# Router logits taken from widened products with the search moved forward, and the experts' inner layer produced transposed from copied weights

## The chip, the cores and the metric

The kernel runs on one core of one Trainium2 chip. The metric is device time in microseconds of one execution, the median of three runs. All arithmetic of interest is fp32. In the rows PE is TensorE (its weight loads are a row of their own, PEld), DVE is VectorE, ACT is ScalarE, POOL is GpSimd, and SP is the engine that issues most transfers.

## The reference, cut to what matters

The input is 8 sequences of 1024 tokens with 128 channels. An attention layer over each sequence is followed by a state-space layer, and then by a mixture of 8 experts of which each token takes the best 2. What the change touches is the end of the second layer and the third:

```python
t = t + _L1_attn_ref(_ln_t(t), ...)      # ends in: x + einsum('ble,de->bld', y, W_out), y 256 wide
t = t + _L1_ffn_ref(_ln_t(t), ...)
# _L1_ffn_ref, on n = 8192 tokens of 128 channels, 8 experts, inner width 341
logits = flat @ router_w.T
probs = softmax(logits); topk_probs, topk_idx = top_k(probs, 2)
topk_probs = topk_probs / (sum(topk_probs) + 1e-09)
h1 = einsum('nc,ehc->neh', flat, w1); h3 = einsum('nc,ehc->neh', flat, w3)
h = silu(h1) * h3
y = einsum('neh,ech->nec', h, w2); out = einsum('ne,nec->nc', gates, y)
```

`_ln_t` is a normalisation over channels, (v - mean) / sqrt(var + 1e-5).

## The kernel before, in words

Every engine runs its own instruction list, written out by hand; semaphores order them, and nothing but the order in the code and the waits decides who runs when.

**The batch stage.** The 8192 tokens are 64 tiles of 128 rows, in 8 batches (sequences) of 8 tiles. `batches` calls `step(base, i)` for 79 steps, `i` from 0 to 7 and `base` the first tile of the batch. A step is a software pipeline: it does the scores of tile i (L346 to L348), the softmax on ACT (L613), the attention output of tile i-1 (L427), the input products of the second layer for tiles i-3 and i-4 (L354, L357, L467, L469), the state-space work of tile i-6 and the end of that layer for tile i-7 (L371 to L375, the output product L432, the residual sum `T2`, L1155). Its mean and variance (L1162, L1183) give `rs2` in `norm_for_experts` on POOL, once a batch at the end of step 6.

**The router.** The finished batch is searched two batches after its first tile. In step 7 and in step 0 ACT normalises its 8 tiles into `XA` (`normed`, L691). In step 0 PE transposes them (`rows_of_x`, L310, two times four into the bank `pc`), ACT copies each half to `VT` (L696), and PE multiplies each tile by the router's weights (`logits`, L316, eight products of 8 columns, each of two instructions). DVE copies the result (L1196) at the end of step 0. In step 1 come the maximum and the softmax (`below_max`, `shares`), the best values (`best`, L948) and their indices (`best_index`, L955); in step 2 the one-hots and gates and, on PE, the counts (L444, L447); in step 3 the rows' places (`places`, `rows`). Then POOL scatters the 16 tiles by `scatter_rows` (L896) to `rows_by_expert` in DRAM, spread over steps 3 to 1 of the next batch by the table `SPREAD`, whose key is (step, place in the step).

**The tables.** After the last step DVE works out which expert each of 136 slots of 128 rows belongs to (L1228 to L1252); the experts of six slots are packed into one number in `TBI`.

**The expert stage.** A loop over 136 slots, four to a loop turn (`group`). SP fetches the slot's rows (`GX`, L273). For slot n PE does, in this order: h1 (L520, the transposed rows stationary, the expert's 341 columns of `W1` moving, into `pX`), the transpose of slot n+1's rows (L509), the three transposes of the gated h of slot n-1 (L529), h3 (L522, likewise with `W3`, into `pY`), and the result of slot n-2 (L537, three chunks of the inner width, `HT` times `W2`). Every fp32 product is two instructions with two weight loads, a transpose is one. ACT copies the transposed rows (L706), takes silu(h1) (L710) and scales the result by the gate (L719). DVE multiplies silu(h1) by h3 (`gated`, L1257), copies the transposed h from `pc` to `HT` (`turned`, L1261), and takes the row numbers and gates (L1268, L1269). POOL scatters each result (L908). At the start of a loop turn PE reads the packed number (`experts_of`) to address `W1`, `W3` and `W2`. At the end SP loads the results back and DVE adds them (L1285, L1287).

## Time and profile before

| | us |
|---|---|
| median of 3 runs (lowest, highest) | 1275.35 (1275.05, 1277.6) |
| the profiled execution's own time | 1275.21 |
| its span, first to last instruction | 1273.4 |
| batch stage and the router's tail, about | 0 to 885 |
| tables and fetch of the first rows, about | 885 to 912 |
| expert stage, about | 912 to 1229 |
| results back, sums, stores, about | 1229 to 1273 |
| mean granted TensorE clock | 0.942 of full |

The profile shows one execution. Busy shares of PE are not a measure of its limit, since its instructions overlap in the records: what counts is the distance from one start to the next. The waits name who released an engine, the chain of waits follows back from the last instruction what each step waited for.

### The profile page before, as it was taken

How to read it: one execution, taken by the hardware profiler on the slowest of the kernel's cores; microseconds unless marked ns; L12 is line 12 of the kernel's file. 1: busy time of each engine (PE TensorE's matmuls, PEld its weight loads, DVE VectorE, ACT ScalarE, POOL GpSimd, SP SyncE). 2: the span in 40 equal slices, each digit the busy share in tenths (PEclk: the TensorE clock that was granted, in tenths of full speed). 3: DMA queues.
4: the chain of work that ended last, by engine and by line, in shares of the span. 5: the costliest groups of instructions: out<-in, count | busy, mean ns of one | idle time of the engine just before them, and what ended most of it. 6: DMA issues, size and time to landing. Idle time of an engine off the chain costs nothing.

```text
span 1273.4 us, 28242 instructions
## 1 busy us (share of the span) xinstructions
PE 1108.5 (87%) x7784; PEld 963.3 (76%) x7785; DVE 866.5 (68%) x2843; ACT 702.8 (55%) x1748; POOL 601.8 (47%) x860
## 2 busy tenths in 40 slices
PE   3899999999999999999999998872399999999950
PEld 2689889888888888888888888762288888888740
DVE  2578887888877887887888777754255555555534
ACT  1576776667767677676666666622144444444420
POOL 7123342564565466556457465555444444444320
PEclk8999999999999999999999999875699999999975
DMA  7100000001001001001000000001222222222249
GB/s 216 28 1 26 10 2 26 18 16 37 17 13 39 8 23 39 10 23 39 5 22 15 18 12 14 12 11 34 55 59 58 58 58 58 58 58 58 57 119 305
DMA packets 73174, 55.21 MB, mean 43 GB/s; under 512 B 9797, under 2 KB 67693, under 8 KB 73069
## 3 DMA queue, kind: packets, MB, share of 16 engines
q1 hardware_dynamic: 55437, 32.15, 9.6%
q0 software_dynamic: 8448, 17.45, 4.3%
q10 hardware_dynamic: 9184, 4.33, 1.2%
q8 instruction: 51, 0.84, 0.3%
q14 instruction: 54, 0.44, 0.1%
HBM read 31.21 MB, written 23.22 MB: 43 GB/s over the span
## 4 chain that ended last, share of the span: by engine, by line
PE 53%; DVE 14%; POOL 12%; issue 12%; ACT 5%; DMA 2%; SPq 1%; POOLq 0%; DVEq 0%; ACTq 0%
PE pX L520 6%; PE pY L522 6%; PE pc L371 5%; PE pa L427 4%; PE pb L537 4%; PE pd L537 4%; PE pc L529 4%; POOL rows_by_expert L896 3%; DVE CV L1020 2%; PE pY L333 2%; ACT PR L613 2%; POOL st L878 2%; DVE NM L1041 2%; PE pc L375 1%; PE pa L382 1%
## 5 line engine op out<-in xcount | busy, mean ns | idle before, releaser
L908 POOL DMA_INDIRECT results_by_choice<-YE,DIX x136 | 130.5, 960 | 190.7 <-ACT YE L719 178.4
L1261 DVE COPY V<-pc 128x384 f32<-128x384 f32 x136 | 75.8, 558 | 133.4 <-PE pc L529 132.1
L896 POOL DMA_INDIRECT rows_by_expert<-XA,SL x128 | 142.3, 1112 | 38.0 <-issue 28.1
L371 PEld LDWEIGHTS pc<-XDT,M 128*128 128x128 f32 x1024 | 130.1, 200 | 17.9 <-issue 13.4
L1020 DVE SCALAR_TENSOR_TENSOR CV<-XBC,cw,CV 128x256 f32<-128x256 f32 x288 | 140.5, 540 | 0.2 <-issue 0.2
L371 PE MATMUL pc<-XDT,M 128*128 128x64 f32 x1024 | 127.7, 280 | 10.7 <-DVE OFF L998 10.0
L427 PE MATMUL pa<-V,PT 128*128 128x128 f32 x1024 | 128.1, 278 | 3.6 <-DVE XDT L1077 3.5
L839 POOL TENSOR_TENSOR YG<-Y,SZ 128x256 f32<-128x256 f32 x64 | 46.5, 726 | 172.2 <-DVE Y L1062 170.0
L427 PEld LDWEIGHTS pa<-V,PT 128*128 128x128 f32 x1024 | 120.0, 192 | 9.6 <-issue 5.7
L520 PE MATMUL pX<-W,TA 128*128 x272 | 104.4, 465 | 0.9 <-ACT TA L706 0.7
L522 PE MATMUL pY<-W,TA 128*128 x272 | 101.1, 454 | 0.0
L1041 DVE TENSOR_REDUCE NM<-pX 128x1 f32<-128x1024 f32 x64 | 77.9, 1218 | 33.2 <-PE pX L348 31.5
L585 ACT ACTIVATE PT<-pY 128x1024 f32<-128x1024 f32 x64 | 65.6, 1025 | 52.3 <-PE pY L333 52.3
L1257 DVE TENSOR_TENSOR X<-XT,pY 128x341 f32<-128x341 f32 x136 | 69.4, 510 | 31.4 <-PE pY L522 19.6
L613 ACT ACTIVATE PR<-pX,NM 128x1024 f32<-128x1024 f32 x64 | 70.8, 1107 | 19.8 <-DVE NM L1041 19.7
L1138 DVE TENSOR_TENSOR M<-ED,GT 128x1024 f32<-128x1024 f32 x64 | 78.3, 1224 | 3.0 <-ACT ED L634 2.7
L706 ACT ACTIVATE TA<-pa 128x128 f32<-128x128 f32 x136 | 37.8, 278 | 74.5 <-PE pa L509 74.5
L333 PE MATMUL pY<-ident,PR 128*128 128x128 f32 x512 | 68.3, 277 | 1.5 <-ACT PR L613 1.5
L529 PE MATMUL pc<-ident,X 128*128 128x128 f32 (+1 forms) x408 | 66.9, 273 | 0.0
L537 PEld LDWEIGHTS pb<-W,V 128*128 128x128 f32 (+1 forms) x408 | 56.1, 191 | 14.0 <-issue 1.1
L537 PEld LDWEIGHTS pd<-W,V 128*128 128x128 f32 (+1 forms) x408 | 56.1, 191 | 12.9
L529 PEld LDWEIGHTS pc<-ident,X 128*128 128x128 f32 (+1 forms) x408 | 50.5, 145 | 20.4 <-DVE X L1257 0.6
(250 smaller groups left out, 2902.9 us busy)
## 6 DMA issues: line engine op xcount, KB each, us to landing
GX<-rows_by_expert SPq DMA_DIRECT2D x136, 65.0 KB
XT<-in_xT_dram SPq DMA_DIRECT2D x8, 512.0 KB, 3.9
X<-in_x_dram SPq DMA_DIRECT2D x16, 256.0 KB, 3.0
W<-results_by_choice SPq DMA_DIRECT2D x8, 512.0 KB, 8.7
out_dram<-T ACTq DMA_DIRECT2D x8, 512.0 KB, 7.3
results_by_choice<-YE,DIX POOLq DMA_INDIRECT x136, 2.2
rows_by_expert<-XA,SL POOLq DMA_INDIRECT x128
W<-in_w1T_dram SPq DMA_DIRECT2D x1, 1364.0 KB
```

Of the source, the lines that this page charges most:

```text
L333: last = nc.tensor.transpose(pY[:, P * j:P * j + P], PR[:, P * j:P * j + P], ident[:])
L371: mm(pc[:, 64 * h:64 * h + 64], M[:, h, :], XDT[:, e % 2, HD * h:HD * h + 64], start=h == 0, stop=False, skip_group_check=True)
L427: last = mm(pa[:, 0:C], PT[:, P * j:P * j + P], V[:, j, :], start=j == 0, stop=j == NT - 1)
L520: mm(pX[:, 512 * par:512 * par + HID], GXT[:, par, :], W1[:, cols], start=True, stop=True).then_inc(s("h1_ps"), 1)
L522: mm(pY[:, 512 * par:512 * par + HID], GXT[:, par, :], W3[:, cols], start=True, stop=True).then_inc(s("h3_ps"), 1)
L529: last = nc.tensor.transpose(pc[0:hn, P * k:P * k + P], HH[:, par, h0:h0 + hn], ident[:])
L537: last = mm((pd, pb)[par][:, 0:C], HT[0:hn, par, k, :], W2[0:hn, bass.ds(expert, 1), k, :], start=k == 0, stop=k == len(HC) - 1)
L613: A(PR[:], pX[:], ACT.Exp, bias=NM[:, i:i + 1], accum_out=RS[:, i:i + 1]).then_inc(s("exp_ready"), 1)
L896: g.indirect_dma_start(xg, bass.IndirectOffsetOnAxis(ap=SL[:, j // NT, j % NT:j % NT + 1], axis=0), XA[:, j // NT, j % NT, :], None).then_ ...
L908: g.indirect_dma_start(yg, bass.IndirectOffsetOnAxis(ap=DIX[:, j, :], axis=0), YE[:, j, :], None).then_inc(s(f"ye{j}_scattered"), 16)
L1020: return stt(CV[:, m, :], XBC[:, m, fo + tap:fo + tap + 256], cw[:, m, tap:tap + 1], CV[:, m, :], ALU.mult, ALU.add)
L1041: v.tensor_reduce(NM[:, i:i + 1], pX[:], AX.X, ALU.max, negate=True).then_inc(s("nm_ready"), 1)
```

## The change

It has three parts.

1. *The logits.* The router's weights become 8 more columns of two products that are done anyway: of `wz` (z of the normalised input, 264 to 272 columns) and of `wo` (the layer's output product, 128 to 136 columns; the 8 are W_out times the router's weights, worked out once in step 3 of the first batch, with two transposes, five small products and three DVE copies, for the first of which PE waits). DVE scales the 8 columns per tile (`XR`, and `LR` beside the residual sum), and in step 7 turns them into logits with the mean and the variance of the normalisation (`logits`, `centred`, `logits_max`, `below`). `rows_of_x`, the old `logits`, `VT`, both ACT copies and the DVE copy of `LG` go.
2. *The search moved forward.* Logits, maximum and exponential run in step 7, the sums, shares and best values in step 0, the indices stay in step 1, the rest in steps 2 and 3. `norm_for_experts` is split, seven tiles ahead of POOL's own `norm` of step 6 and one behind it; the scatters of `SPREAD` lie at fewer places, all behind the small POOL operations of `RY`; `normed` of step 0, `TR`, `take_q` and `take_ql` change their place in the order. `st` gets two buffers.
3. *The experts.* h1 and h3 come out transposed: the weights are stationary (three chunks of 128, 128 and 85 columns) and the 128 transposed rows move. The weights are first copied to a static place `WS`, `W1`'s 341 columns by ACT and `W3`'s by DVE, for each slot; both read the packed number for it. `hidden_T` and `turned` go, the gated product is written straight to `HT` (384 columns), and the result of slot n-1 follows h3 of slot n.

```diff
-            def rows_of_x(base, grp):
-            def logits(base):
...
-                    mm(pb[:, 0:DI + H], XNT[:, 0:P], wz[:], start=True, stop=True).then_inc(s("z_ps"), 1)
+                    mm(pb[:, 0:DI + H + E], XNT[:, 0:P], wz[:], start=True, stop=True).then_inc(s("z_ps"), 1)
...
-                        last = mm(pb[:, 0:C], YT[:, m, :], wo[:, m, :], start=m == 0, stop=m == 1)
+                        last = mm(pb[:, 0:C + E], YT[:, m, :], wo[:, m, :], start=m == 0, stop=m == 1)
...
+                if base == 0 and i == 3:
+
+                    for m in range(2):
+                        last = nc.tensor.transpose(pd[:, P * m:P * m + P], wo[:, m, 0:C], ident[:])
+                    last.then_inc(s("woT_ps"), 1)
+                    pe.wait_ge(s("woT_ready"), 1)
+                    for m in range(2):
+                        mm(pd[:, 256 + E * m:256 + E * m + E], SQ[:, P * m:P * m + P], rT[:], start=True, stop=True, skip_group_check=True)
+                    mm(pd[:, 256 + 2 * E:256 + 3 * E], ones[:], rT[:], start=True, stop=True, skip_group_check=True).then_inc(s("woR_ps"), 1)
...
-                if routes:
-                    upto(pe, "vT_ready", base, -12)
-                    rows_of_x(base, 1)
...
-                if routes:
-                    logits(base)
...
-            def hidden(n, par, expert, between):
+            def hidden(n, par, between):
 
                 pe.wait_ge(s("gxt_ready"), n)
-                cols = bass.ds(expert * HID, HID)
-                mm(pX[:, 512 * par:512 * par + HID], GXT[:, par, :], W1[:, cols], start=True, stop=True).then_inc(s("h1_ps"), 1)
+                pe.wait_ge(s("w1_ready"), n)
+                for k, (h0, hn) in enumerate(HC):
+                    last = mm(pX[0:hn, 512 * par + P * k:512 * par + P * k + P], WS[:, par, 0, h0:h0 + hn], GXT[:, par, :], start=True, stop=True, skip_group_check=True)
+                last.then_inc(s("h1_ps"), 1)
                 between()
-                mm(pY[:, 512 * par:512 * par + HID], GXT[:, par, :], W3[:, cols], start=True, stop=True).then_inc(s("h3_ps"), 1)
-
-            def hidden_T(n, par):
+                pe.wait_ge(s("w3_ready"), n)
+                for k, (h0, hn) in enumerate(HC):
+                    last = mm(pY[0:hn, 512 * par + P * k:512 * par + P * k + P], WS[:, par, 1, h0:h0 + hn], GXT[:, par, :], start=True, stop=True, skip_group_check=True)
+                last.then_inc(s("h3_ps"), 1)
...
+            def weights(par, expert):
+
+                A(WS[:, par, 0, :], W1[:, bass.ds(expert * HID, HID)], ACT.Copy).then_inc(s("w1_ready"), 1)
...
-            SPREAD = {(3, 3): (0, 1), (4, 1): (2,), (4, 2): (3,), (5, 1): (4,), (5, 2): (5,), (6, 1): (6,), (6, 2): (7,),
-                      (7, 1): (8,), (7, 2): (9,), (7, 3): (10,), (0, 1): (11,), (0, 2): (12,), (0, 3): (13,), (1, 1): (14,), (1, 2): (15,)}
+            SPREAD = {(3, 3): (0, 1), (4, 2): (2, 3), (5, 2): (4, 5, 6, 7), (7, 2): (8, 9, 10), (0, 2): (11, 12), (1, 2): (13, 14, 15)}
...
+                        ts(XR[:, (fb + j) % NT, :], bank[:, DI + H:DI + H + E], st[:, fpar, 6, j:j + 1], st[:, fpar, 6, 2 + j:3 + j], ALU.mult, ALU.mult)
...
+                    stt(LR[:, e % NT, :], pb[:, C:C + E], RY[:, 1, 0:1], XR[:, e % NT, :], ALU.mult, ALU.add)
...
-                tt(HH[:, par, :], SH[:, par, :], pY[:, 512 * par:512 * par + HID], ALU.mult).then_inc(s("hh_ready"), 1)
-
-            def turned(n, par):
-                dve.wait_ge(s("hT_ps"), n)
-                v.tensor_copy(HT[:, par].rearrange("p k t -> p (k t)"), pc[:, 0:P * len(HC)]).then_inc(s("hT_ready"), 1)
+                tt(HT[:, par].rearrange("p k t -> p (k t)"), SH[:, par, :], pY[:, 512 * par:512 * par + HP3], ALU.mult).then_inc(s("hh_ready"), 1)
+
+            def weights(par, expert):
+
+                v.tensor_copy(WS[:, par, 1, :], W3[:, bass.ds(expert * HID, HID)]).then_inc(s("w3_ready"), 1)
```

## Rows read from the trace of the kernel before

**Rows 1.** The page: busy time by engine, and the chain that ended last by engine.

```profile
PE 1108.5 (87%) x7784; PEld 963.3 (76%) x7785; DVE 866.5 (68%) x2843; ACT 702.8 (55%) x1748; POOL 601.8 (47%) x860
PE 53%; DVE 14%; POOL 12%; issue 12%; ACT 5%; DMA 2%; SPq 1%; POOLq 0%; DVEq 0%; ACTq 0%
```

**Rows 2.** Busy time in windows: window, length, each engine, PE clock, DMA share, GB/s.

```profile
199.90:203.40 3.50, 3.50 (x13) 2.92 (x12) 1.90 (x5) 2.26 (x6) 2.01 (x5) 0.52 0.00 0
202.64:690.78 488.14, 468.29 (x3552) 421.39 (x3551) 407.07 (x1364) 340.03 (x808) 272.01 (x408) 0.99 0.06 21
...
920.00:1240.00 320.00, 305.57 (x1882) 246.18 (x1880) 162.52 (x539) 132.89 (x401) 130.50 (x136) 0.98 0.24 63
```

**Rows 3.** Timeline of DVE: start and length of L1041, which runs once a step.

```profile
90.66 1.23 DVE L1041 TENSOR_REDUCE NM<-pX 128x1 f32<-128x1024 f32 x1
103.25 1.23 DVE L1041 TENSOR_REDUCE NM<-pX 128x1 f32<-128x1024 f32 x1 [0.57 <-PE pX L348]
185.71 1.22 DVE L1041 TENSOR_REDUCE NM<-pX 128x1 f32<-128x1024 f32 x1
202.62 1.23 DVE L1041 TENSOR_REDUCE NM<-pX 128x1 f32<-128x1024 f32 x1 [1.49 <-PE pX L348]
690.76 1.21 DVE L1041 TENSOR_REDUCE NM<-pX 128x1 f32<-128x1024 f32 x1
```

**Rows 4.** Chain of waits, two stretches: start, length, engine, tile, line, instructions.

```profile
195.43 0.44 PE pc L310 x4
196.73 1.83 PE pc L316 x16
...
938.12 0.67 PE pd L537 x6
```

**Rows 5.** Timeline of PE in the expert stage, one slot, the first of a loop turn.

```profile
1050.21 0.83 PE L520 MATMUL pX<-W,TA 128*128 x2
1050.88 0.27 PE L509 MATMUL pa<-ident,GX 128*128 128x128 f32 x1
1050.99 0.49 PE L529 MATMUL pc<-ident,X 128*128 128x128 f32 x3
1051.32 0.74 PE L522 MATMUL pY<-W,TA 128*128 x2
1051.89 0.83 PE L537 MATMUL pd<-W,V 128*128 x6
1052.56 0.74 PE L520 MATMUL pX<-W,TA 128*128 x2
```

**Rows 6.** Single lines: count, shortest/median/longest ns, first and last start.

```profile
L520 PEld LDWEIGHTS pX<-W,TA x272: 186/190/333, 913.4 to 1221.6; 128*128 128x128 f32 x136
L686 ACT ACTIVATE XA<-XA x8: 1043/1050/1057, 223.0 to 880.1; 128x1024 f32<-128x1024 f32 x8
L1209 DVE TENSOR_SCALAR wx<-wx,pcol x1: 407/407/407, 19.5 to 19.5; 128x384 f32<-128x384 f32 x1
L1054 DVE TENSOR_TENSOR dts<-pb,hrow x32: 147/156/160, 51.9 to 819.9; 128x8 f32<-128x8 f32 x32
```

**Rows 7.** Expert stage by line: busy us, mean ns, then idle before and its releasers.

```profile
L908 POOL DMA_INDIRECT results_by_choice<-YE,DIX x136 | 130.5, 960 | 190.7 <-ACT YE L719 178.4 <-issue 12.2
...
L1261 DVE COPY V<-pc 128x384 f32<-128x384 f32 x134 | 74.7, 558 | 132.2 <-PE pc L529 130.9 <-issue 1.3
L1257 DVE TENSOR_TENSOR X<-XT,pY 128x341 f32<-128x341 f32 x134 | 68.4, 510 | 11.7
L710 ACT ACTIVATE XT<-pX 128x341 f32<-128x341 f32 x133 | 59.9, 450 | 0.2 <-PE pX L520 0.2
```

**Rows 8.** Waits of the batch stage, 90 to 800 us: total us, times, longest.

```profile
PE pb L405 <- POOL YG L839: 12.7, 8, 3.2
```

**Rows 9.** Timeline of the router's tail behind the last batch.

```profile
877.64 0.96 POOL L896 DMA_INDIRECT rows_by_expert<-XA,SL  x1 [0.30 <-issue]
...
884.58 0.17 DVE L1004 CAST SL<-SLF 128x16 uint32<-128x16 f32 x1
```

More of the change, by code:

```diff
@@ L648, in step @@
                     A(DEC[:, dpar], R1b[:], ACT.Exp).then_inc(s("dec_exp"), 2)
-                if routes:
-                    rows_of_x(base, 1)
+                if front_b:
+                    upto(act, "t2_ready", base, fb - 6)
+                    for j in range(2):
+                        last = A(TR[:, fb % NT + j, :], TA[:, fb % NT + j, :], ACT.Identity, bias=st[:, (fb // 2) % 2, 5, j:j + 1], scale=st[:, (fb // 2) % 2, 6, j:j + 1])
+                    last.then_inc(s("tr_ready"), 2)
+                if i in (4, 6) and there(base, NT):
+                    take_q(base + NT, [i // 6])
                 if front_b:
@@ L855, in step @@
                 scatters(2)
+                if i == 6 and there(base, -NT):
+                    norm_for_experts(base, 0, NT - 1)
                 if i == 3 and there(base, -2 * NT):
@@ L946, in best, with shares, best_index @@
+            def shares(b):
+                routing[b].settle()
+                routing[b].did(tt(PB[:], PB[:], bc(r8[:, 2, :]), ALU.mult))
+            def best(b, js):
+                routing[b].settle()
                 apart(dve)
-                for j in range(NT):
+                for j in js:
                     last = v.max(M8[:, j, :], PB[:, j, :])
-                routing[base].then(last)
-            def best_index(base, js):
+                routing[b].did(last)
+            def best_index(b, js):
+                routing[b].settle()
@@ L1105, in step @@
                     steps.did(stt(dts[:, 8], dts[:, 7], ATANH[3], dts[:, 6], ALU.add, ALU.mult))
+                if i == 0 and routes:
+                    best(b, range(4, NT))
+                if front_b:
                     steps.settle()
@@ L1118, in step @@
                     tt(R1b[:], TOT, CUM, ALU.subtract).then_inc(s("dec_in"), 2)
-                if i == 1 and routes:
-                    best_index(base, range(3))
+                if i == 7 and there(base, -NT):
+                    logits(base)
                 if decays:
```

290 lines of the change are left out of this document (149 added, 141 removed).

## The prediction

> **What bounds the kernel now.** I read the page first, then the windows, the timeline of one repeated DVE instruction as a step clock, the chain of waits, and the timeline of one slot of the expert stage. PE carries 53% of the chain that ended last and is busy 87% [rows 1]; the reader should see that no other engine carries more than 14%. In the batch stage DVE is the second: busy 407.07 of 488.14 us, 83%, against PE's 468.29 [rows 2]. So PE work taken out there shows, but only until DVE is met.
>
> L1041 runs once a step. A batch without routing takes 185.71 - 90.66 = 95.05 us, the five with routing behind it (690.76 - 185.71)/5 = 101.01 [rows 3]. Of the 5.96 us between them the greater part lies in step 0: 202.62 - 185.71 = 16.91 us with logits, 103.25 - 90.66 = 12.59 without [rows 3].
>
> In the expert stage PE never rests. From the start of one h1 to the next it is 1052.56 - 1050.21 = 2.35 us, and the pieces fill it: h1 0.67, the rows' transpose 0.11, three transposes of h 0.33, h3 0.57, the result 0.67 [rows 5]. Over 135 slots the mean is (1221.6 - 913.4)/135 = 2.283 us [rows 6], so this slot, the first of its loop turn, is longer than its fellows by (2.35 - 2.283) x 4/3 = 0.09: that is all that shows of the loop branch and of the read of the packed experts. ACT (132.89 us) and DVE (162.52 us) are under 51% busy there [rows 2].
>
> **Part 3, the experts, is the first term.** Six PE instructions of 128 columns with their weight loads take 0.67 us, 0.112 each [rows 4]. h1 and h3 become six such each, as the result already is; the h transposes go; one transpose stays at 0.11 [rows 5]. The slot is 3 x 0.67 + 0.11 = 2.12 us, plus 0.02 for the 0.09 of a loop turn spread over four: 2.14. The gain is 0.143 us x 136 = 19.4 us. Note how little of the 0.33 is left: 384 columns instead of 341, and short loads, give back 0.10 in h1's and h3's place each (0.67 against 0.57).
>
> What hides the copies: ACT's busy time per slot is 132.89/136 = 0.98 us [rows 2]. The copy of `W1` is SBUF to SBUF, 341 columns; the nearest row is 1050 ns for 1024 columns on ACT [rows 6], and silu of 341 from PSUM takes 450 [rows 7]; it costs between 0.45 and 1.05, and I take 0.49, near the row of the same width. silu grows by 43 columns, 0.04. ACT is at 1.5 of 2.14 us (2.1 at the upper bound). DVE: 162.52/136 = 1.20 [rows 2], less `turned` 0.56 [rows 7], plus 0.06 for the wider product, plus the copy of `W3`: 0.41 for 384 columns SBUF to SBUF [rows 6], at most 0.51, the product of the same width [rows 7]. DVE is at about 1.1 to 1.2, no more than now. Both copies are for the slot after the current one, so PE waits for them only if an engine is late by most of a slot. The three added reads of the packed number (on ACT and DVE) have no row on these engines; on PE it shows 0.09 a loop turn. From zero to the 0.5 us per slot that ACT's spare time allows, I take zero.
>
> One handover is left out at the end of the stage (transposes 0.33, `turned` 0.56, two passes between engines, about 0.3): 1.2 us.
>
> The six-instruction row is also where a rule can be weighed. The Trainium skill, "TensorE: Matmul & The Clock Gate", LDWEIGHTS, says that a weight load takes its columns divided by 1.2 in ns, 107 for 128 columns; it speaks against this change, since a load that hid behind 341 moving columns now has only 128 to hide behind. The row, 0.112 us for load and product together, lies 5% over it, so the loads are hidden but with nothing left. By the rule's 0.107 the slot would be 19 x 0.107 = 2.03 and the kernel 15 us faster than I forecast; I stay with the row.
>
> **Parts 1 and 2, the batch stage.** Per routed batch PE loses two times four transposes, 0.44 each, and 16 logit instructions, 1.83 us [rows 4]: 2.71. Right behind the logits, products of 8 columns, PE's clock was at 0.52 for 3.5 us [rows 2]; at half of full speed that costs 1.7 us. The clock's mean of 0.99 over 488 us allows about 10 us at half, three such spells in five batches, so about 1.0 us a batch. The two waits for ACT's copies of `VT` make up the rest of the 4.3 us of step 0. With and without a slow spell I take 3.9 for the mean step 0, and 0.7 for step 1 and after, where PE no longer waits for `LG`.
>
> Added: 8 columns on 264 and on 128, 3% and 6% of instructions of 0.22 and 0.11 us, four of each kind per two and one tile: 0.04 us a tile, 0.35 a batch. DVE gets `XR` and `LR`, two instructions of 8 columns a tile at 156 ns [rows 6], 2.5 us a batch, and five small ones in step 7 in place of two and a copy. DVE's 17% free time [rows 2] is 2.1 us of a step; I let a quarter show, 0.6 (none to all 2.5). The maximum, shares and best values leave step 1 and enter steps 7 and 0, between instructions of chains that wait for one another anyway: nothing. `norm_for_experts`: POOL is late with `YG` once a batch, 12.7 us over 8 times [rows 8]. The split puts one tile's share behind POOL's own norm instead of eight, but adds instructions: nothing to 1.0 gained, I take nothing. Scatters behind `RY` help the residual sum; SP's queue is not moved. Sum per batch: 3.9 + 0.7 - 0.35 - 0.6 = 3.65, for the 7 batches whose step 0 lies in the flow: 25.5 us.
>
> Once, in the first batch, PE waits for DVE's copy of the transposed `wo`, and DVE for five products: two round trips, 0 to 3 us, I take 1.5 lost.
>
> **The tail.** Behind the last tile the new chain saves transposes, copies and logits. But DVE's `both_best` and ACT's copy into `XA` wait for the previous batch's last scatter, issued at 877.64, and the places are ready at 884.58 [rows 9]. The same eight scatters remain to be done behind the norm, so they become the late thing: I take 2 us of gain (0 to 6.9, the distance between those rows). Tables, 16 scatters and the first fetch follow unchanged.
>
> **Sum.** 1273.4 - 19.4 - 1.2 - 25.5 + 1.5 - 2 = 1226.8 us of span. The profiled execution has 1275.21 - 1273.4 = 1.8 around it, and stands 0.1 under the median of the runs: 1228.7, forecast 1228.5.
>
> **The rivals.**
>
> A, the expert slot does not shrink. With 341 columns an instruction lasted 0.29 us (half of 0.57) and PE's own reads at a loop turn were covered by it; now nothing queued lasts longer than 0.112. If a loop turn shows 0.6 us instead of 0.09, the slot is 2.27, the gain 2 us: 1246. For it: the cover is really thinner; against: six short instructions already stand ahead of the read today and it shows 0.09.
>
> B, DVE takes PE's place in the batch stage. It was at 83%; if all 2.5 us of `XR` and `LR` show and the search costs in steps 7 and 0 what step 1 saves, a batch gains about 0.7 and not 3.65: 25.5 becomes 5, and the time 1249.
>
> C, the batch stage gives all. If the routed batch comes down to the 95 us of the unrouted one, 6.0 x 7 = 42: 1212. For it: scatters behind `RY`, `YG` earlier, no slow spells. Against: one-hots, counts and places stay in steps 2 and 3.
>
> D, the end on the other side: DVE becomes the expert stage's bound. Its copy of `W3` would wait for POOL's scatter of 960 ns [rows 7], and the read of the packed number would stop it 0.5 us: 1.2 + 0.96 + 0.5 = 2.66 us a slot, 51 us more than now, with the rest 1228.5 + 19.4 + 51 = 1299. It decides from 2.283 + 27.2/136 = 2.48 us a slot on (27.2 being what the other terms give). Against it: POOL rests 190.7 us before its 136 scatters [rows 7], and ACT takes the other copy.
>
> The Trainium skill, "SBUF — State Buffer", Who interferes with whom, has the rule behind D: VectorE in a two-port mode (an fp32 copy within SBUF among them) and GpSimd exclude one another for a whole instruction. No row of the expert stage shows such a pair, since every wide DVE operand there lies in PSUM today.
>
> **How the numbers follow.** Forecast 0.55 (own range 1219 to 1238); A 0.12; B 0.14; C 0.12; D 0.04; 0.03 for A and B together, 1266, or an end near today's. The range from 1211 to 1250 holds C's centre, A and B, and leaves out some 15%. 0.2% is about what this measurement can tell, 2.5 us; faster 0.94, the same 0.02, slower 0.04.
>
> **What would show it.** Right: L520's successor every 2.12 to 2.15 us with no idle; the sums over L1041 97 to 98 us per routed batch, step 0 near 13; the clock without the spell behind step 0; the first scatter of the last batch about 2 us earlier. Wrong: gaps of PE at each fourth slot (A), PE waiting for DVE at L357 or L439 (B), DVE copies of 1 us and more (D).

## The result, and the profile after

| kernel | runs | median, lowest to highest (us) | profiled span |
|---|---|---|---|
| before | 6 | 1275.91, 1275.05 to 1277.60 | 1273.4 |
| changed | 6 | 1268.85, 1268.52 to 1272.17 | 1267.0 |

The ratio is 0.995, interval 0.9936 to 0.9963: 7 us faster, outside the range of 1211 to 1250 that was given, and 40 us above the forecast. One execution of e19 below took 2276.7 us, and one of the kernel before beside it 1940.0; the medians leave these two out.

The page of the changed kernel, busy time by engine and the chain that ended last by engine (before: [rows 1]):

```profile
PE 1076.8 (85%) x8280; PEld 991.7 (78%) x8281; DVE 856.0 (68%) x2991; ACT 739.3 (58%) x1869; POOL 626.4 (49%) x972
PE 45%; DVE 17%; issue 13%; POOL 13%; ACT 7%; DMA 3%; SPq 1%; ACTq 0%; POOLq 0%; DVEq 0%; another core or an unknown queue 0%
```

PE is busy 32 us less in a program that got 6.4 us shorter: the work went and the time didn't. PE's share of the chain falls from 53% to 45%, while DVE's, POOL's, ACT's and "issue" rise.

Four marks cut the span: the last `T2` (end of the batch stage), the last `SL` (places known), PE's second transpose of fetched rows, and its last.

| stretch | before | changed | difference | forecast |
|---|---|---|---|---|
| start to last `T2` | 863.8 | 881.2 | +17.4 | -24.0 |
| last `T2` to last `SL` | 20.8 | 17.9 | -2.9 | -2 |
| `SL` to second transpose | 30.1 | 30.1 | 0 | 0 |
| second to last transpose, 134 slots | 305.3 | 285.6 | -19.7 | -19.4 |
| last transpose to end | 53.5 | 52.2 | -1.3 | -1.2 |

Four of five stretches are as forecast to within 1 us. The batch stage has the wrong sign.

One slot of the changed kernel's expert stage (before: [rows 5]), PE alone: start, length, line.

```profile
1043.75 0.83 PE L513 MATMUL pX<-TA,XBC 128*128 128x128 f32 x6
1044.41 0.27 PE L506 MATMUL pa<-ident,GX 128*128 128x128 f32 x1
1044.52 0.83 PE L518 MATMUL pY<-TA,XBC 128*128 128x128 f32 x6
1045.19 0.83 PE L526 MATMUL pb<-W,V 128*128 x6
1045.86 0.83 PE L513 MATMUL pX<-TA,XBC 128*128 128x128 f32 x6
```

From start to start: 0.66, 0.11, 0.67, 0.67, and the slot is 2.11 us, as nearly everywhere: 129 of the 134 distances from transpose to transpose lie between 2.10 and 2.12, so no fourth slot is longer. The copies beside it, by line (before: [rows 7]): count, busy, mean ns, idle before.

```profile
L1294 DVE TENSOR_TENSOR V<-XT,pY 128x384 f32<-128x384 f32 x127 | 70.4, 555 | 132.0 <-ACT XT L690 110.4 <-PE pY L518 18.9 <-remote 1.4
L686 ACT ACTIVATE XBC<-W 128x341 f32 x128 | 63.6, 497 | 7.2 <-issue 7.1
L690 ACT ACTIVATE XT<-pX 128x384 f32<-128x384 f32 x127 | 61.6, 485 | 0.0
L1298 DVE COPY XBC<-W 128x341 f32 x127 | 46.0, 362 | 28.1 <-issue 28.0
```

ACT copies `W1` in 497 ns (forecast 490), DVE copies `W3` in 362 (forecast 410 to 510; the longest of all 136 takes 534).

Now the batch stage, by the same once-a-step instruction as [rows 3], L1060 now:

```profile
98.46 1.21 DVE L1060 TENSOR_REDUCE NM<-pX 128x1 f32<-128x1024 f32 x1
111.05 1.23 DVE L1060 TENSOR_REDUCE NM<-pX 128x1 f32<-128x1024 f32 x1 [0.57 <-PE pX L344]
...
197.80 1.23 DVE L1060 TENSOR_REDUCE NM<-pX 128x1 f32<-128x1024 f32 x1 [1.17 <-PE pX L344]
210.52 1.23 DVE L1060 TENSOR_REDUCE NM<-pX 128x1 f32<-128x1024 f32 x1 [0.57 <-PE pX L344]
...
709.88 1.23 DVE L1060 TENSOR_REDUCE NM<-pX 128x1 f32<-128x1024 f32 x1 [0.16 <-PE pX L344]
```

Step 0 with routing is 210.52 - 197.80 = 12.72 us, as short as without (111.05 - 98.46 = 12.59): the 3.9 us were gained in full. Yet five routed batches take (709.88 - 197.80)/5 = 102.4 us each, 1.4 more than before, and the one without routing 99.34, 4.3 more. The first begins 7.8 us later. So the search and the scatters can't be the whole loss: a batch that has neither lost most.

Step by step (differences of the starts of L1041 or L1060, the middle value of the five routed batches):

| step | 0 | 1 | 2 | 3 | 4 | 5 | 6 | 7 |
|---|---|---|---|---|---|---|---|---|
| before | 16.9 | 11.9 | 11.9 | 12.3 | 11.8 | 11.1 | 11.7 | 13.8 |
| changed | 12.7 | 13.2 | 12.1 | 12.6 | 12.2 | 12.4 | 12.1 | 14.9 |

Windows of the changed kernel (the long one answers to the second of [rows 2]), and the instruction at which PE went on at 393.55:

```profile
197.91:709.99 512.08, 477.55 (x3557) 429.24 (x3556) 428.97 (x1491) 345.87 (x826) 294.48 (x490) 0.98 0.07 21
390.00:393.00 3.00, 1.17 (x15) 0.94 (x13) 0.40 (x2) 2.51 (x8) 2.58 (x11) 1.00 0.00 0
393.00:396.00 3.00, 2.45 (x13) 2.45 (x14) 3.00 (x13) 2.03 (x6) 2.56 (x5) 0.63 0.00 0
396.00:399.00 3.00, 3.00 (x18) 2.72 (x18) 2.84 (x10) 0.86 (x5) 2.40 (x2) 0.80 0.09 28
393.55 0.50 PE L401 MATMUL pb<-ident,YG 128*128 128x128 f32 x2 [2.38 <-POOL YG L833]
```

PE is busy 93% now where it was 96%. In step 7 it stands idle 2.38 us, waiting for `YG`, and then the granted clock falls from 1.00 to 0.63 and 0.80, that is, it stands at its lower level, 1.2 GHz, for (0.37 + 0.20) x 3 / 0.5 = 3.4 us, which costs 1.7. In windows of 3 us over the whole stage such a spell follows step 7's gap (2.36 to 2.54 us) in each of the six batches from 189 to 705 us, and there is no other. Those of the kernel before lie elsewhere, in step 0 with routing, right behind the products of 8 columns and without a gap: PE was busy all of the windows around them, at 198 to 204, 399 to 405, 600 to 609 and 705 to 711 us. Two of these windows:

```profile
402.00:405.00 3.00, 3.00 (x12) 2.43 (x10) 1.15 (x5) 2.26 (x6) 2.01 (x4) 0.53 0.00 0
603.00:606.00 3.00, 3.00 (x10) 2.42 (x10) 1.64 (x6) 2.06 (x6) 1.84 (x4) 0.50 0.03 8
```

In the changed kernel none of the windows of step 0 from 197 to 723 us is under 0.99. So the old spells went with the products, as forecast, and the new ones came with the gap.

Who waits, 90 to 800 us (before: [rows 8], and 3.5 us for `XDT` in 9 waits):

```profile
PE pb L401 <- POOL YG L833: 16.2, 13, 2.5
PE pa L420 <- DVE XDT L1093: 12.8, 17, 1.2
```

Both waits end in one chain. The timeline at the turn from step 6 to 7 of one batch, the instructions of that chain alone:

```profile
384.98 0.75 DVE L920 SCALAR_TENSOR_TENSOR QL<-pX,pcol,QH 128x512 fp32r<-128x512 f32 x1 [0.18 <-ACT QH L558]
385.65 0.28 DVE L1196 BATCH_NORM_STATS2 BN<-TA 128x6 f32<-128x128 f32 x1
...
386.08 0.18 DVE L1209 BATCH_NORM_AGGREGATE MV<-BN 128x2 f32<-128x6 f32 x1
...
386.74 1.35 POOL L872 TENSOR_SCALAR NMN<-MV 128x2 f32<-128x2 f32 x1
386.78 1.25 DVE L1041 SCALAR_TENSOR_TENSOR CV<-XBC,cw,CV 128x256 f32<-128x256 f32 x3
387.96 1.20 DVE L1060 TENSOR_REDUCE NM<-pX 128x1 f32<-128x1024 f32 x1
388.15 0.19 POOL L873 TENSOR_SCALAR st<-MV 128x2 f32<-128x2 f32 x1
...
390.02 0.20 POOL L878 TENSOR_TENSOR st<-st,NMN 128x4 f32<-128x4 f32 x1
390.18 0.19 POOL L796 TENSOR_TENSOR rs<-NMN,MV 128x1 f32<-128x1 f32 x1
390.26 0.88 ACT L579 ACTIVATE XN<-TA,st 128x128 f32<-128x128 f32 x2 [2.99 <-POOL st L878]
...
391.25 1.10 ACT L594 ACTIVATE PR<-pX,NM 128x1024 f32<-128x1024 f32 x1
...
392.78 0.72 POOL L833 TENSOR_TENSOR YG<-Y,SZ 128x256 f32<-128x256 f32 x1
392.80 0.42 DVE L1093 TENSOR_TENSOR XDT<-pa,DT 128x256 f32<-128x256 f32 x1 [2.60 <-ACT GT L603]
```

`QL` now stands ahead of `BN`, so `MV` comes 0.75 us later; POOL's norm then begins just as DVE starts three conv products, and its second instruction, two values per partition, takes 1.35 us where its neighbour takes 0.19. ACT stands idle 2.99 us ahead of `XN`, for the end of the norm. `PR` stands behind `XN` in ACT's queue and starts 2.1 us after its maximum is done (389.16). `GT`, `XDT` and, behind eight more POOL instructions, `YG` follow late, though `Y` was ready at 390.19.

### The profile page after: what moved, and what is told of

Same layout as the page of the kernel before. It is cut to its first block, busy times and chain, and to the rows that moved or that the text cites. A ratio compares the mean times of both kernels' runs of the same rounds, so it can differ in the third digit from the quotient of the medians.

```text
span 1267.0 us, 29808 instructions
## 1 busy us (share of the span) xinstructions
PE 1076.8 (85%) x8280; PEld 991.7 (78%) x8281; DVE 856.0 (68%) x2991; ACT 739.3 (58%) x1869; POOL 626.4 (49%) x972
## 4 chain that ended last, share of the span: by engine, by line
PE 45%; DVE 17%; issue 13%; POOL 13%; ACT 7%; DMA 3%; SPq 1%; ACTq 0%; POOLq 0%; DVEq 0%; another core or an unknown queue 0%
PE pX L513 7%; PE pY L518 6%; PE pa L420 5%; PE pc L367 4%; PE pb L526 3%; PE pd L526 3%; POOL st L874 3%; DVE CV L1041 2%; POOL st L873 2%; POOL rows_by_expert L893 2%; ACT PR L594 2%; PE pY L329 2%; PE pc L468 1%; PE pa L378 1%; POOL NMN L872 1%
## 5 line engine op out<-in xcount | busy, mean ns | idle before, releaser
L1294 DVE TENSOR_TENSOR V<-XT,pY 128x384 f32<-128x384 f32 x136 | 75.4, 555 | 141.1 <-ACT XT L690 118.1
L420 PE MATMUL pa<-V,PT 128*128 128x128 f32 x1024 | 139.2, 293 | 13.4 <-DVE XDT L1093 12.8
L420 PEld LDWEIGHTS pa<-V,PT 128*128 128x128 f32 x1024 | 130.1, 206 | 20.7 <-issue 18.3
L367 PEld LDWEIGHTS pc<-XDT,M 128*128 128x128 f32 x1024 | 127.8, 197 | 20.7 <-issue 16.2
L1041 DVE SCALAR_TENSOR_TENSOR CV<-XBC,cw,CV 128x256 f32<-128x256 f32 x288 | 138.6, 534 | 0.0
L367 PE MATMUL pc<-XDT,M 128*128 128x64 f32 x1024 | 126.2, 278 | 13.2 <-DVE OFF L1018 10.9
L513 PE MATMUL pX<-TA,XBC 128*128 128x128 f32 (+1 forms) x816 | 114.4, 277 | 1.7 <-ACT TA L682 1.1
L518 PE MATMUL pY<-TA,XBC 128*128 128x128 f32 (+1 forms) x816 | 113.7, 276 | 0.0
L1060 DVE TENSOR_REDUCE NM<-pX 128x1 f32<-128x1024 f32 x64 | 77.9, 1216 | 34.6 <-PE pX L344 30.2
L513 PEld LDWEIGHTS pX<-TA,XBC 128*128 128x128 f32 (+1 forms) x816 | 97.8, 181 | 2.3 <-ACT TA L682 1.6
L518 PEld LDWEIGHTS pY<-TA,XBC 128*128 128x128 f32 (+1 forms) x816 | 97.7, 181 | 0.0
L594 ACT ACTIVATE PR<-pX,NM 128x1024 f32<-128x1024 f32 x64 | 70.8, 1106 | 19.8 <-DVE NM L1060 19.7
L686 ACT ACTIVATE XBC<-W 128x341 f32 x136 | 67.6, 497 | 20.4 <-issue 20.3
L579 ACT ACTIVATE XN<-TA,st 128x128 f32<-128x128 f32 x64 | 28.2, 488 | 84.2 <-POOL st L878 84.2
L1093 DVE TENSOR_TENSOR XDT<-pa,DT 128x256 f32<-128x256 f32 x64 | 27.2, 424 | 72.9 <-ACT GT L603 72.9
```

Source lines behind the costliest of these rows:

```text
L367: mm(pc[:, 64 * h:64 * h + 64], M[:, h, :], XDT[:, e % 2, HD * h:HD * h + 64], start=h == 0, stop=False, skip_group_check=True)
L420: last = mm(pa[:, 0:C], PT[:, P * j:P * j + P], V[:, j, :], start=j == 0, stop=j == NT - 1)
L513: last = mm(pX[0:hn, 512 * par + P * k:512 * par + P * k + P], WS[:, par, 0, h0:h0 + hn], GXT[:, par, :], start=True, stop=True, skip_grou ...
L518: last = mm(pY[0:hn, 512 * par + P * k:512 * par + P * k + P], WS[:, par, 1, h0:h0 + hn], GXT[:, par, :], start=True, stop=True, skip_grou ...
L594: A(PR[:], pX[:], ACT.Exp, bias=NM[:, i:i + 1], accum_out=RS[:, i:i + 1]).then_inc(s("exp_ready"), 1)
L1041: return stt(CV[:, m, :], XBC[:, m, fo + tap:fo + tap + 256], cw[:, m, tap:tap + 1], CV[:, m, :], ALU.mult, ALU.add)
```

## The experiments

All were run with the kernel before beside them. "Last `T2`" is the start of the last `T2` instruction in each profile: the batch stage alone.

| run | what it is | median (us) | ratio to before, 95% | last `T2` |
|---|---|---|---|---|
| e1b | before + new experts | 1251.9 | 0.9800 to 0.9833 | 863.7 |
| e2b | changed, old experts | 1296.1 | 1.0152 to 1.0196 | 881.9 |
| e3b | changed, old order of ACT and DVE | 1252.8 | 0.9804 to 0.9839 | 867.0 |
| e4b | changed, old plan of POOL | 1277.6 | 1.0010 to 1.0037 | 888.8 |
| e5 | changed, `take_ql` back | 1241.6 | 0.9717 to 0.9757 | 854.8 |
| e6 | changed, old scatter places | 1281.3 | 1.0024 to 1.0050 | 891.5 |
| e7 | e3b + early one-time products | 1249.0 | 0.9769 to 0.9819 | 863.1 |
| e8 | e3b without `XR`, `LR` | 1242.7 | 0.9717 to 0.9767 | 855.6 |
| e9 | before, `take_ql` forward | 1298.9 | 1.0166 to 1.0203 | 886.0 |
| e10 | e5 + early one-time products | 1240.2 | 0.9703 to 0.9747 | 854.7 |
| e11 | e10 + one-hots later | 1234.8 | 0.9661 to 0.9699 | 853.3 |
| e14 | e1b + new scatter places | 1249.7 | 0.9781 to 0.9812 | 860.8 |
| e12 | e11, norm undivided | 1238.3 | 0.9692 to 0.9722 | 853.6 |
| e13 | e11, `XR` behind `Y` | 1239.5 | 0.9713 to 0.9752 | 853.9 |
| e16 | changed, conv products later | 1235.8 | 0.9690 to 0.9731 | 850.1 |
| e17 | e5 + conv products later | 1226.8 | 0.9598 to 0.9631 | 843.3 |
| e18 | all that paid | 1222.3 | 0.9568 to 0.9616 | 835.5 |
| e19 | e1b + conv products later | 1247.1 | 0.9742 to 0.9788 | 857.8 |

### Which part of the change (e1b, e2b)

e1b puts the new `hidden`, `result`, `weights`, `silu`, `gated` and `experts_of` into the kernel before; e2b puts the old ones into the changed kernel.

```diff
-                mm(pX[:, 512 * par:512 * par + HID], GXT[:, par, :], W1[:, cols], start=True, stop=True)
+                for k, (h0, hn) in enumerate(HC):
+                    last = mm(pX[0:hn, ...], WS[:, par, 0, h0:h0 + hn], GXT[:, par, :], ...)
```

> The kernel before with the experts' part of the change alone (transposed h1 and h3, weights copied by ACT and DVE), router as before. The traces give the stage from the first h1 to the end of the kernel as 360.0 us before (913.4 to 1273.4) and 339.2 after (927.8 to 1267.0), 20.8 less. Theory 1 (the parts are independent, the batch stage gave the loss): 1275.9 - 20.8 = 1255.1 us. Rival (the loop is fast only because something of the new router lets it be, or the batch stage's loss came with the added tensors): 1262 or more.

> The changed kernel with the experts' stage of before: only the router's part of the change. Theory 1: the whole loss is in it, 1268.9 + 20.8 = 1289.7 us, 14 us slower than before. Rival (the two parts disturb one another): 1276 to 1283.

e1b: 1251.9, 23.5 us faster than before. e2b: 1296.1, 20.8 slower. The batch stages end at 863.7 and 881.9, as in the kernel before (863.8) and the changed one (881.2): the parts are independent, and the router's part costs 17 us (by e1b) to 21 (by e2b).

### Whose order (e3b, e5, e9)

e3b restores the order of both queues (on ACT, `TR`, `take_q` and `normed`), e5 that of one instruction on DVE; e9 makes the same move, reversed, in the kernel before.

```diff
-                if i in (4, 6) and there(base, NT):
-                    take_ql(base + NT, [i // 6])
                 if there(base, o):
...
                     v.bn_stats(BN[:, o % NT, :], TA[:, o % NT, :]).then_inc(s("bn_ready"), 1)
...
                     v.bn_aggr(MV[:, o % NT, :], BN[:, o % NT, :]).then_inc(s("mv_ready"), 1)
...
+                if i in (4, 6) and there(base, NT):
+                    take_ql(base + NT, [i // 6])
```

> The changed kernel with the order of before in two queues: ACT does CV before TR and take_q, and the first normed group of step 0 early; DVE does take_ql behind bn_aggr. Theory O (the new places delay XN and XDT by way of mv_ready and POOL's norm): steps 4, 5 and 6 of a batch, which grew by 0.4, 1.3 and 0.4 us, come back, 2.1 x 7 = 15 us: 1254 us. Rival L (the added small instructions of DVE and POOL cost it, wherever the rest stands): 1266 to 1272, no difference. Third possibility: the new places were a gain by themselves, and the time is 1275.

> The changed kernel with one instruction moved back: DVE's take_ql (0.75 us) behind bn_aggr again, ACT's order left as changed. Theory Q: this one place is what delays mv_ready, POOL's norm, XN, and with it PR, XDT and YG of steps 5 and 7, and so it alone gives most of the 16 us that the old order of both queues gave: 1253 to 1257 us. Rival A: ACT's new order (TR and take_q ahead of CV) is the costly part, and the time stays at 1265 to 1269. Both half: 1261.

> The kernel before with that one instruction moved alone: take_ql ahead of the bn_stats, as in the change. Theory Q (the place costs whatever else is changed: MV comes 0.75 us or more later, POOL's norm then begins beside DVE's three conv products and one of its small operations takes 1.35 instead of 0.2 us, XN holds PR back on ACT): 27 us were lost by it in the changed kernel, so 1290 to 1300 us. Rival: it needs the added POOL work of the change behind the norm; alone the delay is covered by the wait for YG that stands there anyway: 1275 to 1280.

e3b: 1252.8, as theory O said. But e5, with less moved, is at 1241.6: one instruction of 0.75 us, used twice a batch, cost 27 us, and ACT's new order, which e3b had undone along with it, is a gain of 11 (why, no run asks). e9: 1298.9, 24 us slower than before, so the place costs the same in the old kernel; there steps 5 and 7 grow to 12.3 and 15.5 us, and the batch without routing to 99.2, the changed kernel's 99.3. And the spells of step 7 belong to this place: e9 has them too, at 183, 285, 390, 600 and 705 us, and in e5 no window from 90 to 620 us is under 0.99.

The same turn of steps in e5:

```profile
372.22 0.17 DVE L1207 BATCH_NORM_AGGREGATE MV<-BN 128x2 f32<-128x6 f32 x1
372.31 0.75 DVE L920 SCALAR_TENSOR_TENSOR QL<-pX,pcol,QH 128x512 fp32r<-128x512 f32 x1
...
372.86 0.19 POOL L872 TENSOR_SCALAR NMN<-MV 128x2 f32<-128x2 f32 x1
...
373.48 1.26 DVE L1041 SCALAR_TENSOR_TENSOR CV<-XBC,cw,CV 128x256 f32<-128x256 f32 x3
...
374.85 1.23 DVE L1060 TENSOR_REDUCE NM<-pX 128x1 f32<-128x1024 f32 x1
374.99 0.20 POOL L878 TENSOR_TENSOR st<-st,NMN 128x4 f32<-128x4 f32 x1
375.22 0.88 ACT L579 ACTIVATE XN<-TA,st 128x128 f32<-128x128 f32 x2 [0.91 <-POOL st L878]
376.22 1.09 ACT L594 ACTIVATE PR<-pX,NM 128x1024 f32<-128x1024 f32 x1
```

The norm is through at 375.19, 0.34 us after the maximum starts; in the changed kernel it was 390.22 - 387.96 = 2.26. `PR` starts 0.14 us after its maximum is done instead of 2.1. Here the norm's first three instructions pass before the conv products begin (the next one, L874, began 0.02 us ahead of them and took the 1.02 us that it takes in the changed kernel). They don't everywhere. Of the 32 norms, this many have an instruction of over 1.1 us among the first three, each beside conv products: 28 in the changed kernel, 15 in e5, 9 before, 22 in e9.

```profile
L873 POOL TENSOR_SCALAR st<-MV x32: 192/1334/1343, 42.3 to 819.5; 128x2 f32<-128x2 f32 x32
```

### Delay or collision (e16, e17)

```diff
-                    for m in range(3):
-                        last = conv(2, m)
...
                     v.tensor_reduce(NM[:, i:i + 1], pX[:], AX.X, ALU.max, negate=True)
+                if decays:
...
+                    for m in range(3):
+                        last = conv(2, m)
```

> The changed kernel as it is (take_ql forward, 1268.9 us), with DVE's three conv products of odd steps (1.26 us) behind the maximum instead of ahead of it. POOL's norm behind steps 4 and 6 then finds no conv product beside it, but the maximum, which reads PSUM. Theory C (the stretch of one POOL instruction from 0.2 to 1.35 us is the greater part of the 27 us): most of it comes back, 1245 to 1253. Rival Q (the 0.75 us and the queue behind it): what comes back is only what the earlier maximum gives by itself, the same as in the companion kernel with take_ql back, 0 to 5 us: 1264 to 1269.

> The companion: take_ql back (1241.6 us), conv products of odd steps behind the maximum. By theory C there is little stretch left here (the median of that POOL instruction is 0.19 us), so the time moves only by what an earlier maximum and a later SX chain give: 1237 to 1245. If it falls by as much as its companion does, the companion shows nothing of the stretch.

e16 gains 33.0 us and e17 14.9. e17's fall is more than I gave it, so the companion must be subtracted: 33.0 - 14.9 = 18 of the 27 us that the place of `QL` cost go when POOL's norm no longer meets the conv products, and 9 remain (1235.8 - 1226.8) for the delay itself. In e5 half of the collisions were still there (15 of 32 norms), and e17 has 1; 14 x 1.16 = 16 us, an estimate, is about what it falls. In e16, `QL` still forward:

```profile
374.11 0.18 DVE L1210 BATCH_NORM_AGGREGATE MV<-BN 128x2 f32<-128x6 f32 x1
...
374.76 0.19 POOL L872 TENSOR_SCALAR NMN<-MV 128x2 f32<-128x2 f32 x1
375.02 0.19 POOL L873 TENSOR_SCALAR st<-MV 128x2 f32<-128x2 f32 x1
...
375.57 1.23 DVE L1056 TENSOR_REDUCE NM<-pX 128x1 f32<-128x1024 f32 x1 [0.69 <-PE pX L344]
376.58 0.19 POOL L876 TENSOR_SCALAR st<-st 128x2 f32<-128x2 f32 x1 [0.20 <-POOL st L874]
```

None of the norm's first three instructions is stretched (1 of the 32 norms in e16); its last, L878, which now meets the conv products, takes 0.38 us instead of 0.20. The counts give the split a second way: the place of `QL` adds 13 collisions (28 - 15, and 22 - 9 in the kernel before), of 1.35 - 0.19 = 1.16 us each, and 14 delays of 0.75, an estimate of 15 + 10.5 = 26 us, if all of it shows, for the 27 and 24 measured. The split by runs has a weak side: moving the conv products also brings the maximum 1.2 us earlier, and what that is worth may differ between the two kernels.

### POOL's plan (e4b, e6, e14, e12)

```diff
-            SPREAD = {(3, 3): (0, 1), (4, 2): (2, 3), (5, 2): (4, 5, 6, 7), (7, 2): (8, 9, 10), ...}
+            SPREAD = {(3, 3): (0, 1), (4, 1): (2,), (4, 2): (3,), (5, 1): (4,), (5, 2): (5,), (6, 1): (6,), ...}
...
-                if i == 6 and there(base, -NT):
-                    norm_for_experts(base, 0, NT - 1)
...
-                    norm_for_experts(base, NT - 1, NT)
+                    norm_for_experts(base, 0, NT)
```

e6 has the first hunk, e12 the second (on e11), e4b both; e14 puts the new places into e1b.

> The changed kernel with POOL's old plan: scatters spread over 15 places as before, and the experts' norm undivided behind POOL's norm of step 6. Theory P (the pairs and fours of scatters at one place and the divided norm hold YG back: waits for YG of 10.7 us in four batches against 5.8, and PE's clock falls to half behind that wait in each batch): 1.2 us of waiting and up to 1.5 us of slow clock a batch come back, 2.7 x 7 = 19 us: 1250. Rival: the added pool instructions themselves (rs2's third row and the first norm's product), not their places: 1266 to 1270.

> The changed kernel with the scatters over 15 places as before, the experts' norm divided as changed. Together the two old ways of POOL cost 8.7 us (1277.6 against 1268.9). Theory S: the places of the scatters matter, 1275 or more, since four of them leave the stretches ahead of XW and YG. Rival N: the divided norm is the gain (its 1.5 us pow and six small instructions stood between POOL's norm and YG, the wait for YG is 2.5 us and grew to 3.6), and the time stays within 2 us of 1268.9.

> The kernel before with the experts' part and the change's places for the scatters (1251.9 us without these places). In the changed kernel the old places cost 12.4 us. Theory S (the places pay by themselves, since none stands ahead of XW or of POOL's norm of step 6 any more): 1240 to 1245 us. Rival (they pay only beside the changed router, whose norm for the experts stands in step 6 twice): 1250 to 1253. If S is right, the kernel with the old router stands beside the one with the new router in its best order, and the new logits are worth next to nothing.

> The best kernel so far (take_ql back, early one-time products, one-hots behind SX: 1234.8 us) with the experts' norm undivided, behind POOL's norm of step 6. With the old scatter places the undivided norm was 3.7 us faster than the divided one (1277.6 against 1281.3). Theory N (the divided norm doubles seven small POOL instructions and its pow): 1231 us. Rival (the undivided one puts a 1.5 us pow ahead of YG in step 7, where the divided one has 0.57): 1239 to 1242.

My theory P was wrong: the changed plan is a gain. Old places cost 12.4 us (e6), both old ways 8.8 (e4b). In the old router the new places give 2.2 us (e14), which is within the spread of the runs (1247.6 to 1250.1 against 1249.5 to 1252.4), so they pay beside the longer POOL work of the changed router. The division has no sign of its own: undivided is 3.7 faster with the old places (e4b against e6) and 3.5 slower in e12, whose last `T2` differs by 0.3 us only. These 3.5 us lie within the spread of either kernel's runs (1235.7 to 1239.2, 1232.8 to 1237.9); I leave it open.

### The one-time products (e7, e10)

In e7 and e10 the transposes stand in step 1 and the products in step 2 of the first batch:

```diff
-                if base == 0 and i == 3:
+                if base == 0 and i == 1:
+                    pe.wait_ge(s("setup"), 1)
                     for m in range(2):
                         last = nc.tensor.transpose(pd[:, P * m:P * m + P], wo[:, m, 0:C], ident[:])
...
+                if base == 0 and i == 2:
                     pe.wait_ge(s("woT_ready"), 1)
```

The changed kernel around them, PE and DVE:

```profile
45.81 3.50 PE L420 MATMUL pa<-V,PT 128*128 128x128 f32 x16
49.14 0.38 PE L436 MATMUL pd<-ident,wo 128*128 128x128 f32 x2
...
50.34 0.39 DVE L1212 COPY SQ<-pd 128x256 f32<-128x256 f32 x1
50.78 0.61 PE L440 MATMUL pd<-rT,SQ 128*128 128x8 f32 x4 [1.26 <-DVE SQ L1212]
...
51.48 0.68 PE L466 MATMUL pY<-XNT,wx 128*128 128x256 f32 x2
```

From 49.14 to 51.48 is 2.3 us, the round trip; L420 takes 3.50 us there, and 1.95 one step earlier and at this place in the kernel before, where the clock stayed at 1.00. It is at 0.61, 0.83, 0.74 and 0.69 from 45 to 57 us: it fell ahead of the one-time products, behind a stretch from 43.5 to 45 us in which PE did nothing.

> The changed kernel with the old order of both queues (1252.8 us), and the one-time products of w_out and the router's weights cut in two: transposes in step 1, products in step 2 of the first batch, where PE has nothing to do, instead of one round trip in step 3. The first batch takes 73.2 us against 67.1 before the change, 5.5 of it in step 3. Theory: the round trip with the slow clock behind it is that term, and it goes: 1252.8 - 5.5 = 1247.3 us. Rival: something else holds step 3 (DVE's added instructions, a slow clock behind the wait for XN that comes anyway): 1250 to 1253.

> The changed kernel with take_ql back behind bn_aggr (1241.6 us), and the one-time products cut in two and put in steps 1 and 2 of the first batch. Its first batch takes 71.3 us, against 67.1 before the change. With the old queue order the same cut gave 3.8 us (73.2 to 69.3 in the batch): 1238 us if the term is the same; 1241 if the slow clock behind XN's wait comes back by itself.

e7: 3.8 us less by the medians, and its first batch takes 69.3 instead of 73.2. e10: 1.5 us less, the batch 69.8 instead of 71.3. Both gains lie within the spread of the runs (e7 1247.5 to 1254.8, e3b 1248.4 to 1254.3), but both profiles have the same step shorter, 13.5 to 7.9 and 11.9 to 9.5 us. The round trip is a term of about 2 to 4 us; the full 5.5 that I expected of e7 hold what a slow clock adds, and that comes and goes with other gaps of this batch.

### DVE's added work (e8, e13, e11)

`XR` takes 280 ns and `LR` 218, not the 156 of the nearest row:

```profile
L1071 DVE TENSOR_SCALAR XR<-pb,st x32: 267/280/281, 58.4 to 835.5; 128x8 f32<-128x8 f32 x32
L1189 DVE SCALAR_TENSOR_TENSOR LR<-pb,RY,XR x64: 207/218/226, 95.7 to 881.1; 128x8 f32<-128x8 f32 x64
```

e8, on e3b:

```diff
-                        ts(XR[:, (fb + j) % NT, :], bank[:, DI + H:DI + H + E], ...)
-                    stt(LR[:, e % NT, :], pb[:, C:C + E], RY[:, 1, 0:1], XR[:, e % NT, :], ...)
```

> The changed kernel with the old order of both queues (1252.8 us), and the 64 XR and 64 LR instructions left out; LR is filled once from the router's weights, so the logits are not the reference's. It prices DVE's added work: XR lasts 0.28 and LR 0.22 us, 0.5 us a tile, 4.0 us a batch. Theory B (DVE, at over 83% busy, gives PE's gain away): a good part shows, 1.5 to 3 us a batch over 7 batches, 1252.8 - 10 to 21 = 1232 to 1242 us. Rival: these two stand beside waits and cost nothing: 1250 to 1253. By my forecast's quarter: 1 us a batch, 1246.

e13, on e11:

```diff
-                        ts(XR[:, (fb + j) % NT, :], bank[:, ...], ...)
                         tt(dts[:, 0, j, :], bank[:, DI:DI + H], hrow[:, 0, :], ALU.add)
...
                     last.then_inc(s("y2_ready"), 1)
+                        ts(XR[:, (fb + j) % NT, :], (pb, pd)[j][:, ...], ...).then_inc(s("u_ready"), 1)
```

> The best kernel so far (1234.8 us) with the two XR instructions of a step behind Y instead of ahead of it. XR lasts 0.28 us, so Y and YG come 0.5 us earlier in four steps of eight. Leaving XR and LR out gave 10 us in all. Theory (their place ahead of Y is the greater part, PE waits for YG 10.9 us in 13 waits): 5 to 8 us, 1227 to 1230. Rival (the same time is only passed on to the softplus chain and XDT behind Y): 1233 to 1237.

e8 fills `LR` once, so its logits aren't the reference's: it serves as a price only. It gives 10.1 us, 3.9 of them in the first batch (73.2 to 69.3) and about 0.9 in each routed one (100.1 to 99.2): a fifth of their 4.0 us shows. e13 is 4.7 slower than e11 by the medians, and its routed batches take 99.1 instead of 98.0, though its last `T2` comes only 0.6 later: no gain in any of these, so the place ahead of `Y` isn't what costs.

e11, on e10:

```diff
-                if i == 2 and routes:
-                    one_hots(b)
...
                     stt(SX[:, par]..., ALU.add, ALU.mult).then_inc(s("sx_ready"), 2)
+                if i == 2 and routes:
+                    one_hots(b)
```

> As the kernel with take_ql back and the early one-time products (1238 us expected), and in step 2 the one-hots (four DVE instructions, 1.2 us) behind the maximum and SX instead of ahead of them. Theory D (DVE works without a pause from 306.6 to 318.6 us, through steps 1 and 2, and PE waits there once a batch 1.1 us for CTP, which hangs on the maximum and SX): PR and CTP come 1.2 us earlier, 0.8 to 1.1 us a batch, 1231 us. Rival: the delay only moves to SZ, XR, Y and YG behind them, or to the counts that wait for the one-hots: 1237 to 1240.

e11: 1234.8, 5.4 us less than e10; PE's wait for `CTP` between 196 and 790 us falls to 0.2 us. In e10 it was

```profile
PE pa L378 <- ACT CTP L598: 6.8, 7, 1.1
```

Between e10 and e11 the waits for `YG` rise from 5.2 to 10.9 us: a good part comes back there.

### All of it, and the old router beside it (e18, e19)

> The changed kernel with all that paid: take_ql back behind bn_aggr, conv products of odd steps behind the maximum (together 1226.8 us), one-time products in steps 1 and 2 (1.5 us alone) and one-hots behind SX (5.4 us beside the old place of the conv products). If they add: 1226.8 - 1.5 - 5.4 = 1220 us. If the one-hots' gain is already in the earlier maximum (PE's wait for OFF fell to 0.6 us with the conv products moved, the wait for CTP did not, 6.5 us in seven): 1222 to 1226.

> The kernel before with the experts' part (1251.9 us) and the conv products of odd steps behind the maximum, old router and old scatter places. In the changed router the same move gave 14.8 us with take_ql back. Theory: POOL's stretched operations are the old kernel's too (one of the three lasts up to 1.34 us in its trace), 1236 to 1243 us. Rival: in the old router step 1's search stands between, and POOL was rarely stretched there (median 0.19 us): 1246 to 1252. The distance to the kernel with all corrections is what the new router is worth when both stand in a good order.

e18 takes `take_ql` back, the early products, the later one-hots and the later conv products together: 1222.3, 52 us (4.1%) faster than before, the fastest of all. The one-hots' gain is partly in the earlier maximum, as the second case had it. e19: 1247.1, the rival's range. The old router gains 4.8 us by the move that gives the new one 14.9, and the new one is 25 us faster beside it (e18), 20 without the later one-hots and the early products (e17). The forecast had 24 for the batch stage and 2 for the tail. This distance isn't the logits' alone: e19 has neither ACT's new order, worth 11 us in the changed router, nor the new scatter places, and what the first would give the old router was not run.

## Why the prediction was wrong

**The experts, right.** Slot forecast 2.14, measured 2.13 on the mean and 2.11 in a turn; gain 19.4, measured 19.7; end 1.2 and 1.3. Both copies came out as priced. Rivals A (a loop turn that shows 0.6 us) and D (DVE late) did not occur: PE shows no gap between slots. By the rule of the Trainium skill that I weighed ("TensorE: Matmul & The Clock Gate", LDWEIGHTS), the slot would have been 2.03; the measurement is nearer to the row, 0.111 us for load and product together. The load alone doesn't set this pace: two of h1's six loads have 85 columns and not 128, which the 19 x 0.107 passed over, yet h1 takes the 0.66 us of the result with its six full ones. Rival D's copy of `W3` never came near 1 us (534 ns at most); its reading that every wide DVE operand of the stage lay in PSUM was wrong, `gated` read silu(h1) from `XT` in SBUF.

**"3.9 for the mean step 0", right.** 16.5 on the mean of the five batches before, 12.7 after. The clock's share was right in kind: step 0 took 16.9 to 17.1 us in the three of these batches with a spell behind the products of 8 columns and 15.8 in the two without, 0.7 on the mean where I had 1.0, and the spell went with the products. What I didn't foresee are the new spells behind the gap in step 7.

**"Search leaves step 1", wrong in size.** I took 0.7 us gained for step 1 and after; step 1 grew by 1.3 and step 2 by 0.2. From 214.5 to 236 us, most of steps 1 and 2, DVE is busy 20.7 of 21.5 us, so what PE gave up in step 0 it waits for there. e11 names the place: one-hots ahead of the maximum. This much is rival B, that DVE takes PE's place. (B's 0.7 us a batch doesn't follow from its terms: 3.65 less 1.9 for `XR` and `LR` less 0.7 for the search is 1.05.)

**`XR` and `LR`, right by two errors.** 4.0 us a batch instead of 2.5, a fifth shown instead of a quarter: 0.9 against 0.6.

**The one-time products**: forecast 1.5, bound 3; the first batch grew by 7.8. The round trip is 2.3 us of it (2 to 4 by e7 and e10); I had left out the slow clock: at 45 us it fell behind an idle stretch, and L420 took 3.50 us instead of 1.95. The kernel before had idle time there too (busy 1.36 of 3 us from 43 to 46) and kept 1.00. What lengthened PE's idle stretch ahead of the one-time products stays open.

**The step that failed is one that the prediction doesn't have.** The change puts `take_ql` ahead of `bn_stats`. I costed what the parts add and remove and named the search, the norm and the scatters as moved; this instruction, which the description of the change lists among those moved, stood at nothing without a reason. It costs 27 us (e5), and 24 in the kernel before (e9). With it undone the kernel stands at 1241.6 us, 13 above the forecast and inside its range: five routed batches gain 101.0 - 98.7 = 2.3 each instead of 3.65, the rest of the stage behind them (the last two) 1.3 together instead of 7.3, and the first batch loses 4.2 instead of 1.5. Why the last two give so little no run shows. By e16 and e17 two thirds of the 27 are a collision on POOL, one third the delay.

The chain could have been followed. What it needed was in the trace of the kernel before: DVE's instruction of 0.75 us, which would now stand ahead of `MV`, POOL's norm behind `MV`, `XN` behind the norm, and `PR`, which PE waits for, behind `XN` on ACT. So was the collision: one of the norm's instructions has a median of 194 ns and a longest of 1343 in the kernel before. I had even cited the rule, as that of rival D, but in half. The Trainium skill, "SBUF — State Buffer", Who interferes with whom, says besides that a VectorE instruction with two SBUF inputs contends with a GpSimd instruction that reads SBUF, and that a `tensor_reduce` never does. The trace agrees in both halves: 1.35 us beside the conv products, whose two wide inputs lie in SBUF, 0.19 beside the maximum, which reads PSUM (L876 in e16, inside the maximum's 375.57 to 376.80).

**The tail, right**: 2.9 against 2, and for the reason given. `both_best` waits 5.51 us for the last scatter of the batch before, and the places are ready at 899.12.

## What to carry to other kernels

In a pipeline held together by queues a moved instruction is a part of the change like an added one: list every one, and follow from each place who stands behind it on its engine and who waits for those, over three engines if need be. Here one of 0.75 us cost 1.9 us at each of its 14 places. And when removed work on the busiest engine brings nothing, look where its idle time went before giving up the idea: the same router, in another order of the queues, stands 25 us below the old one.
